# Decays of two linear-attention stages: broadcast sums and per-head activations instead of bf16 matmuls

## The reference, cut to what matters

```python
dt = softplus(x @ Win.T + dt_bias); g = dt * -exp(A_log_bias)
G = cumsum(g, within the chunk)
scores = q_i . k_j
decay = where(i >= j, exp(G_i - G_j), 0)
y_intra = (scores * decay) @ (v * dt)
y_inter = (q * exp(G)) @ state        # of the chunk before
```

## Time and profile before

| | |
|---|---|
| three executions | 2699.6, 2704.6, 2707.73 us (median 2704.6) |
| the profiled execution | 2708.85 us, of which 2707.1 us is the span |
| TensorE busy | 2567.5 us, 95% |
| VectorE, GpSimd, ScalarE busy | 69%, 53%, 50% |
| mean granted TensorE clock | 0.979 |
| moved by DMA | 118.79 MB, mean 44 GB/s |

### The profile page before, as it was taken

How to read it: one execution, slowest core, us unless ns; L and a number is a source line. 1 busy time by engine, 2 the same in 40 slices (tenths; PEclk the granted TensorE clock), 3 DMA queues, 4 the chain that set the end, 5 groups by cost and what they waited for, 6 DMA issues and landing times.

```text
span 2707.1 us, 58907 instructions
## 1 busy us (share of the span) xinstructions
PE 2567.5 (95%) x19678; PEld 2045.6 (76%) x19678; DVE 1862.9 (69%) x2720; ACT 1363.2 (50%) x2492; POOL 1428.0 (53%) x1404
## 2 busy tenths in 40 slices
PE   4999999999999759899999999999999999999989
PEld 3778787787787538677787787777777877877777
DVE  5675766666757568757677767587576777685864
ACT  3434434334334345656665665665566656656621
POOL 1654655546546110457556656475575566564720
PEclk8999999999999769999999999999999999999999
DMA  2010110110110014211111111101111111111011
GB/s 90 24 50 26 35 44 23 44 40 19 52 36 12 17 59 140 78 45 38 50 33 58 34 41 50 38 30 50 45 38 50 33 58 34 42 49 38 19 46 47
DMA packets 72632, 118.79 MB, mean 44 GB/s; under 512 B 10310, under 2 KB 22214, under 8 KB 72373
## 3 DMA queue, kind: packets, MB, share of 16 engines
q1 hardware_dynamic: 72388, 115.61, 13.1%
HBM read 102.92 MB, written 12.65 MB: 43 GB/s over the span
## 4 chain that ended last, share of the span: by engine, by line
PE 52%; DVE 3%; issue 2%; POOL 2%; ACT 0%; DVEq 0%; POOLq 0%; ACTq 0%
PE proj L218 11%; PE proj L220 11%; PE proj L219 11%; PE core_y L1409 5%; PE core_o L1415 2%; PE decay L1471 1%; PE turned L253 1%; DVE mx_acc L1216 1%; PE turned L1439 1%; PE mx_decay L1471 1%; PE mx_normed L1439 1%; PE mx_normed L253 1%; PE core_y L220 1%; PE core_y L218 1%; PE mx_decay L220 1%
## 5 line engine op out<-in xcount | busy, mean ns | idle before, releaser
L218 PE MATMUL proj<-slab_hi,XTL 128*128 128x512 f32 x816 | 355.3, 435 | 0.0
L201 DVE TENSOR_TENSOR slab_lo<-slab_raw,slab_hi 128x512 fp32r<-128x512 f32 (+2 forms) x272 | 245.5, 915 | 148.7 <-ACT slab_hi L192 123.1
L218 PE MATMUL proj<-XTH,slab_lo 128*128 128x512 f32 x736 | 301.2, 409 | 41.0 <-PEq L81 14.4
L220 PE MATMUL proj<-slab_hi,XTH 128*128 128x512 f32 x816 | 321.1, 393 | 0.0
L219 PE MATMUL proj<-slab_lo,XTH 128*128 128x512 f32 x816 | 318.7, 391 | 0.0
L219 PE MATMUL proj<-XTL,slab_hi 128*128 128x512 f32 x736 | 292.9, 398 | 0.0
L220 PE MATMUL proj<-XTH,slab_hi 128*128 128x512 f32 x736 | 292.9, 398 | 0.0
L1670 POOL TENSOR_TENSOR mx_th<-mx_th,mx_acc 128x512 f32<-128x512 f32 x48 | 62.2, 1296 | 363.4 <-ACT mx_th L1569 363.4
L1687 POOL TENSOR_TENSOR mx_gate<-mx_gate,mx_hd 128x512 f32<-128x512 f32 x128 | 167.9, 1312 | 152.1 <-DVE mx_hd L1601 141.1
L218 PE MATMUL proj<-slab_hi,mx_otl 128*128 128x512 f32 x576 | 242.0, 420 | 4.1 <-DVE mx_otl L267 4.1
L220 PE MATMUL proj<-slab_hi,mx_oth 128*128 128x512 f32 x576 | 227.8, 396 | 0.0
(11 more groups left out here) (358 smaller groups left out, 6667.4 us busy)
## 6 DMA issues: line engine op xcount, KB each, us to landing
slab_raw<-in_w_gate SPq DMA_DIRECT2D x64, 256.0 KB, 3.0
slab_raw<-in_w_out SPq DMA_DIRECT2D x64, 256.0 KB, 3.0
slab_raw<-in_w_x SPq DMA_DIRECT2D x60, 256.0 KB, 3.6
slab_raw<-in_w_q SPq DMA_DIRECT2D x32, 256.0 KB, 3.0
slab_raw<-in_w_g SPq DMA_DIRECT2D x32, 256.0 KB, 3.0
slab_raw<-in_w_o SPq DMA_DIRECT2D x32, 256.0 KB, 2.9
bc_scratch<-bc_acc SPq DMA_DIRECT2D x32, 256.0 KB, 2.0
slab_raw<-in_w_bc SPq DMA_DIRECT2D x20, 256.0 KB, 4.4
```

The costliest lines, as they stand in the source:

```text
L201: op = nc.vector.tensor_tensor(K.SL[par][:, c, 0:width], K.RAW[c][:, 0:width], hi, ALU.subtract)
L218: nc.tensor.matmul(to[:, 0:bh.shape[-1]], al, bh, start=(c == 0), stop=False)
L220: mm = nc.tensor.matmul(to[:, 0:bh.shape[-1]], ah, bh, start=False, stop=(c == KC - 1))
```

## The change

G is stored once, in fp32. For each 128 tokens DMA reads a row of the sums of all heads of the round (4 x 128 values, 2 KB) or half (8 x 128, 4 KB) and writes it to all 128 partitions. G is also turned, so that G_j stands as one column per head (`upto`; in layer 0 also `left` = Glast - G). ScalarE makes Relu(G_j - G_i) head by head, with that column as bias, 128 columns at a time, four such activations in place of one; exp follows as before over four heads. The matmuls, the bf16 parts, the row tiles and their setup go. In layer 1 exp is taken while turned tiles are copied out of two banks. In the mixer four tiles of sums are loaded ahead, the first four before the groups. In the attention the bank of the removed matmuls serves as a second bank for turned tiles, so tile t waits for tile t - 2. The program's scratch for dynamic DMA is set to 4096 bytes. The diff, cut to its core (code that is only removed and stands in the listing above is left out in part; `TB`, `GB` and `bank` arguments are passed on likewise elsewhere):

```diff
@@ -132,31 +132,27 @@
+        sums = [nc.dram_tensor(f"sums{i}", s, F32, kind="Internal").ap() for i, s in enumerate(((NB, 2, H0 * P), (NT, P * P)))]
...
+            dt0, upto0, left0 = (mem.enter_context(nc.sbuf_tensor(n, [P, NT, H0], F32)) for n in ("dt0", "upto_sum0", "to_last0"))
...
+            dt1, upto1 = (mem.enter_context(nc.sbuf_tensor(n, [P, NT, P], F32)) for n in ("dt1", "upto_sum1"))
...
-            K.RHS = [mem.enter_context(nc.sbuf_tensor(f"mx_g_rows{i}", [P, HH1, SEQ], BF16)) for i in range(2)]
-            K.LHS = [mem.enter_context(nc.sbuf_tensor(f"mx_j_rows{i}", [P, 2, SEQ], BF16)) for i in range(2)]
@@ -488,20 +475,15 @@
-            sp.dma_start(stage[:, :], d["head_rows"].rearrange("p h n -> p (h n)")).then_inc(S["mx_rows"], 16)
...
-        for i in range(3):
-            for k in range(kinds):
-                sp.wait_ge(av, HEAD + part_made(i, k))
...
-                    sp.dma_start(rows[0][i].rearrange("b h t -> (b h) t"), parts[i][:, :]).then_inc(st, 16)
...
+        sp.wait_ge(vv, HEAD + G_READY)
+        if layer:
+            sp.dma_start(sums.rearrange("t (h i) -> h t i", i=P), G[:, :].rearrange("h (t i) -> h t i", i=P)).then_inc(st, 16)
+        else:
+            for b in range(NB):
+                sp.dma_start(sums[b].rearrange("c (h i) -> h c i", i=P),
+                             G[b * H0:(b + 1) * H0, :].rearrange("h (c i) -> h c i", i=P)).then_inc(st, 16)
+            sp.wait_ge(st, HEAD + 16 * NB)
@@ -509,35 +491,27 @@
-            for i in range(2):
...
+        if layer == 0:
+            for src, ready, bank in ((q, DT_READY, K.PT), (G, G_READY, K.PD), (R, R_READY, K.PO)):
+                pe.wait_ge(vv, HEAD + ready)
+                for i in range(2):
+                    tr = nc.tensor.transpose(bank[:, i * P:(i + 1) * P], src[:, i * P:(i + 1) * P], K.ident[:, :])
...
-    if layer:
-        @block.gpsimd
-        def _(pool):
-            for i in range(2):
...
-                nc.gpsimd.memset(K.LHS[i][:, :, :], 0.0)
...
-                nc.gpsimd.memset(K.RHS[i][:, :, :], 0.0).then_inc(S["mx_zero"], 1)
...
-            for i in range(2):
...
-                nc.gpsimd.memset(K.LHS[i][0:15, :, :], 1.0)
...
-                rows_set = nc.gpsimd.tensor_copy(K.RHS[i][0:15, :, :].rearrange("p h n -> p (h n)"), stage[:, :])
-            rows_set.then_inc(S["mx_set"], 1)
+        else:
+            for use, (src, ready) in enumerate(((q, DT_READY), (G, G_READY))):
+                pe.wait_ge(vv, HEAD + ready)
+                for i, bank in enumerate((K.PT, K.PD)):
+                    if use:
+                        pe.wait_ge(cc, HEAD + i + 1)
+                    for t in range(4):
+                        at = 4 * i + t
+                        tr = nc.tensor.transpose(bank[:, t * P:(t + 1) * P], src[:, at * P:(at + 1) * P], K.ident[:, :])
+                    tr.then_inc(tt, 1)
+            pe.wait_ge(vv, HEAD + R_READY)
+            pe.wait_ge(cc, HEAD + 3)
+            for b in range(NB):
+                tr = nc.tensor.transpose(K.PT[:, b * P:(b + 1) * P], R[:, 2 * b * P:(2 * b + 1) * P], K.ident[:, :])
+            tr.then_inc(tt, 1)
@@ -560,29 +534,23 @@
-                elif dst is dtk:
...
-        for i in range(3):
-            for k in range(kinds):
...
-                nc.scalar.activation(split3[k][i][:, :], ((G, R) if i == 0 else (z, dd))[k][:, :], ACT.Copy).then_inc(av, 1)
-            if layer and i == 0:
-                nc.scalar.activation(e[:, :], G[:, :], ACT.Exp).then_inc(av, 1)
...
-                nc.scalar.activation(w[:, :], R[:, :], ACT.Exp, scale=-1.0).then_inc(av, 1)
...
+        if layer == 0:
+            for k, (dst, bank, sign) in enumerate(((dtk, K.PT, 1.0), (turned[0], K.PD, 1.0), (turned[1], K.PO, -1.0))):
+                act.wait_ge(tt, HEAD + k + 1)
+                nc.scalar.activation(dst[:, :, :].rearrange("p (b i) h -> p i b h", i=2),
+                                     bank[:, 0:2 * P].rearrange("p (i b h) -> p i b h", i=2, b=NB), ACT.Copy, scale=sign).then_inc(cc, 1)
+        else:
+            upto, from_start, to_end = turned
+            for i, bank in enumerate((K.PT, K.PD)):
+                act.wait_ge(tt, HEAD + i + 1)
+                nc.scalar.activation(dtk[:, 4 * i:4 * i + 4, :], bank[:, :].rearrange("p (t h) -> p t h", t=4), ACT.Copy).then_inc(cc, 1)
+            for i, bank in enumerate((K.PT, K.PD)):
+                src = bank[:, :].rearrange("p (t h) -> p t h", t=4)
+                act.wait_ge(tt, HEAD + 2 + i + 1)
+                nc.scalar.activation(from_start[:, 2 * i:2 * i + 2, :], src[:, 1::2, :], ACT.Exp)
+                nc.scalar.activation(upto[:, 4 * i:4 * i + 4, :], src, ACT.Copy).then_inc(cc, 1)
+            act.wait_ge(tt, HEAD + 5)
+            nc.scalar.activation(to_end[:, :, :].rearrange("p b h -> p (b h)"), K.PT[:, :], ACT.Exp, scale=-1.0).then_inc(cc, 1)
@@ -707,18 +667,16 @@
-            sp.dma_start(stage, d["head_rows"][:, 0:REP0, :].rearrange("p h n -> p (h n)")).then_inc(S["at_ld"], 16)
...
-                sp.wait_ge(S["at_set"], HEAD + 1)
-                sp.wait_ge(K.unit_done, HEAD + U + SLOTS * g)
-                sp.dma_start(RHS[0:3, :, :, :], rd[:, :, ds(REP0 * g, REP0), :]).then_inc(S["at_rows"], 16)
-                for k, src in enumerate((nd, md)):
...
+                sp.wait_ge(S["at_e"], HEAD + PAIRS * g)
+                for b in range(NB):
+                    for it in range(2):
+                        src = sums[b, it:it + 1, ds(REP0 * P * g, REP0 * P)].broadcast_to([P, REP0 * P])
+                        sp.dma_start(GB[b][:, it, :, :].rearrange("p h n -> p (h n)"), src).then_inc(S["at_rows"], 16)
@@ -739,11 +697,7 @@
-                nc.tensor.matmul(PS[k % 2][:, :], KH[:, js], QH[:, :, qs], start=False, stop=True)
-                pe.wait_ge(S["at_rows"], HEAD + 48 * (g + 1))
-                pe.wait_ge(S["at_e"], HEAD + PAIRS * g + k - 1)
-                nc.tensor.matmul(PD[k % 2][:, :], LHS[:, int(p == 1), jt * P:(jt + 1) * P], RHS[:, b, :, (it % 2) * P:(it % 2 + 1) * P],
-                                 start=True, stop=True).then_inc(S["at_pair"], 1)
+                nc.tensor.matmul(PS[k % 2][:, :], KH[:, js], QH[:, :, qs], start=False, stop=True).then_inc(S["at_pair"], 1)
@@ -766,18 +720,16 @@
+                        pe.wait_ge(K.ot_lo, HEAD + m - 5 + s)
...
-                            tr = nc.tensor.transpose(K.PT[:, t * P:(t + 1) * P], vT[:, tt * P:(tt + 1) * P], K.ident[:, :])
+                            tr = nc.tensor.transpose(TB[s % 2][:, t * P:(t + 1) * P], vT[:, tt * P:(tt + 1) * P], K.ident[:, :])
...
-                        turn_tile(nc, K, pe, m + t, GT[t % GRING], K.ot_lo if t else S["at_v"], m + t if t else 2 * g + 2)
+                        free, count = (K.ot_lo, m + t - 1) if t >= 2 else (S["at_v"], 2 * g + t + 1)
+                        turn_tile(nc, K, pe, m + t, GT[t % GRING], free, count, TB[t % 2])
@@ -844,15 +796,23 @@
-                            act.wait_ge(S["at_pair"], HEAD + PAIRS * g + k + 1)
+                            b, p = pairs[k]
+                            jt, it = 2 * b + (p == 2), int(p > 0)
+                            act.wait_ge(S["at_rows"], HEAD + 128 * (g + 1))
...
-                                nc.scalar.activation(ex, PD[k % 2][:, :], ACT.Exp).then_inc(S["at_e"], 1)
...
-                                nc.scalar.activation(ex, PD[k % 2][:, :], ACT.Relu, scale=-1.0).then_inc(S["at_rl"], 1)
-                                act.wait_ge(S["at_rl"], HEAD + 8 * g + 2 * pairs[k][0] + (pairs[k][1] == 2) + 1)
-                                nc.scalar.activation(ex, ex, ACT.Exp, scale=-1.0).then_inc(S["at_e"], 1)
+                            alone(act)
+                            for h in range(REP0):
+                                src, head = GB[b][:, it, h, :], ds(REP0 * g + h, 1)
+                                if p == 1:
+                                    ex = nc.scalar.activation(EX[k % 2][:, h, :], src, ACT.Exp, bias=left[:, jt, head])
+                                else:
+                                    rl = nc.scalar.activation(EX[k % 2][:, h, :], src, ACT.Relu, bias=upto[:, jt, head], scale=-1.0)
+                            if p != 1:
+                                rl.then_inc(S["at_rl"], 1)
+                                act.wait_ge(S["at_rl"], HEAD + 8 * g + 2 * b + (p == 2) + 1)
+                                ex = EX[k % 2][:, :, :].rearrange("p h n -> p (h n)")
+                                ex = nc.scalar.activation(ex, ex, ACT.Exp, scale=-1.0)
+                            ex.then_inc(S["at_e"], 1)
@@ -871,14 +831,7 @@
-            nc.vector.memset(LHS[:, :, :], 0.0)
-            nc.vector.memset(RHS[:, :, :, :], 0.0).then_inc(S["at_zero"], 1)
-            dve.wait_ge(S["at_zero"], HEAD + 1)
-            nc.vector.memset(LHS[0:15, :, :], 1.0)
-            dve.wait_ge(S["at_ld"], HEAD + 64)
-            for b in range(NB):
```

(43 more changed lines are left out.)

121 lines of the change are left out of this document (19 added, 102 removed).

## The result

The changed kernel takes 2685.7 us (median of 6 runs, 2680.5 to 2688.2), the one before 2706.2 us beside it (6 runs). The ratio is 0.992, with a 95% interval of 0.991 to 0.993. It is faster, but by 21 us where 67 were forecast; 2638 was off by 48 us and the time lies above the range. The profiled execution took 2688.24 us.

What follows compares the result with a forecast made beforehand. TensorE, busy 95% of the span, was taken to bound the kernel. Terms -24 - 28 - 8 - 6.5 - 5.9 + 5.5 gave -67 us, so 2704.6 became 2638 us, own range 2622 to 2653, with A and B 2608 to 2668.

Steps and rivals of the forecast that it cites:

- Decay matmuls removed, mixer (-50.7): Mixer's score slots: TensorE saves 0.34 or 0.43 us per removed pair of decay matmuls, 50.7 us over sixteen halves.
- ScalarE's price: Decays by head on ScalarE: four 128-column Relus cost 1.32 us against 0.61 for one of 512, 0.7 more.
- ScalarE's lag (+22): Mixer's score slots: gates queue behind longer decays, making TensorE 1.4 us late per half, 22 us over sixteen halves.
- B: Rival, mixer: ScalarE lags more, at 0.36 us per Relu instead of 0.30; +20 us, 2658 us; chance 0.18.
- C: Rival, mixer: ScalarE becomes the bound, slower than before; 2720 us at 0.46 us per Relu; chance 0.03.
- A: Rival, mixer: ScalarE keeps up, so all 50.7 us of removed matmuls stay; 2616 us; chance 0.18.
- D: Rival: broadcasts clog the DMA queue; 2645 us at half the present rate, near 2710 at a quarter; chance 0.04.
- E: Rival: removed matmuls do not pay, hidden behind another chain; only the three openings count; 2690 us; chance 0.07.
- Attention rounds (-24): Attention rounds: each removed set of decay matmuls saves TensorE 0.24 us, x 96, taken as 24 us.
- Attention's start (-6.5): Attention's start: without memsets and casts the first k's rotation, awaited by the third unit, ends 6.5 us sooner.
- mixer's start (+5.5): Mixer's start: four broadcasts issued before the gate slab delay its first chunk, 5.5 us more, bounds 0 and 12.
- Normalisation c (-8) and decay phase (-5.9): Without row-tile setup GpSimd stops slowing VectorE in normalisation c, 8 us; mixer's decay phase has a shorter chain, 5.9 us.

Runs made afterwards that it cites:

- run 1: Changed kernel with one wide Relu or Exp in place of four by head, per-head bias left out, in attention and mixer: 2648.0 us, 0.978.
- Run 9: The kernel of run 4 with HD and TO of tile 1 moved ahead on VectorE, between the two M multiplies of slot r=3: 2646.1 us, 0.978.
- 14: The kernel of Run 9 with the wide Relu and Exp, per-head bias left out, in both phases: 2640.6 us, 0.976.
- run 11: The kernel of Run 9 with GpSimd's XCH of tile 7 ahead of the sums of squares at r=10: 2653.1 us, 0.979.
- run 2: Changed kernel with the broadcasts loaded once ahead of the loops and never again, later decays computed from those rows: 2686.8 us, 0.994.
- run 3: Changed kernel with both the wide Relu or Exp without per-head bias and the broadcasts loaded once: 2653.5 us, 0.982.
- run 4: Changed kernel with gate slabs loaded ahead of the broadcasts on SP, in attention rounds and at the mixer's start: 2664.9 us, 0.985.
- run 7: Changed kernel with GpSimd's row-tile setup (six memsets, two copies) put back in the second decay phase, into tiles nobody reads: 2694.2 us.
- run 6: Changed kernel with one turned bank in the attention again, with the waits of the kernel before: 2680.9 us, 0.991.

## Why the prediction was wrong, and where it was right

*Decay matmuls removed, mixer (-50.7).* The size was right: with ScalarE's work made cheap (run 1) the 16 intervals are 6.5 us a group shorter than before, 52 in all. In the changed kernel only 2.4 us a group of it can be seen.

*ScalarE's price.* Right. 0.30 from one Relu to the next and 0.39 for the last were taken; the rows after say

```profile
1682.73 1.23 ACT L1484 ACTIVATE mx_decay<-mx_g_all,upto_sum 128x128 f32<-128x128 f32 x4
L1484 ACT ACTIVATE decay<-mx_g_all,upto_sum 128x128 f32<-128x128 f32 x380 | 118.1, 370 | 0.0
```

that four take 1.23 us, so with 0.37 for the last they start 0.29 apart, and the mean is 370 ns. One of 512 columns takes 0.60 (run 1), so four cost 0.63 more, where 0.7 was taken. The estimate from the Trainium skill ("ScalarE: Activation LUTs", What ACT_TABLE_LOAD costs), 294 ns apart, agrees with that spacing.

*ScalarE's lag (+22).* This step failed, and it is most of the miss: the mixer's loop was to be 28 us shorter and is 2.9 longer. Two things were wrong in it.

The first is the path. The forecast followed one chain behind ScalarE, tanh and VectorE's gate multiply, and gave it 1.6 us of slack. It did not follow the other, from ScalarE's exp over the M multiply, tile_lo, HD and TO to GpSimd's two products and the turn of tile 1. That one needs 2.6 us of GpSimd behind VectorE's last instruction and ran out first. Run 9 shows it: moving two instructions along it took the wait away. The expected wait for mx_gate of VectorE was short (2.7 us in all in after). By run 1 ScalarE's work costs at least 4.1 us a group, 33 in all, where 22 were taken. That the two sizes are not further apart is luck, for the 22 stood on the wrong chain and on a wrong sum: three units of 2.8, 1.4, 2.1 and 0.9 make 12.8 us, not 12.2, and by the forecast's own steps the lag would then be 1.1 us a half at most instead of 1.7.

The second is a term put at nothing: chains that have nothing to do with ScalarE, and that held TensorE as soon as it came sooner. GpSimd's full queue takes back 1.35 us a group in interval 43, and 0.8 more go in intervals 18, 19 and 42. The turn of the loop takes back what 45 and 47 gained. A cheaper ScalarE left these as they were (runs 1 and 14), and letting XCH go first moved the loss (run 11). That is 2.2 us a group, 17 in all. What ended the waits at 18, 19 and 42, and the 0.3 us at 12 and 36, was not taken apart.

*Rivals.* The "less than 1 us" a half that was put down for B or C came true, but not by their mechanism: the Relu was not mis-sized, the chains behind it were. A fell, and D did (run 2). E's time, 2690, is 4 us from the measured one, and that is chance: the attention paid, the starts did not. But a part of its mechanism is in the traces, since a third of what the 16 intervals gain without ScalarE's lag is hidden behind GpSimd and the other chains (run 3: 4.5 of 6.4 us a group are left).

*Attention rounds (-24).* 17.8 us with the last round, 2.3 a round. Most of the intervals with a decay are 0.24 us shorter, as read from starts, but not the one before the fourth score (interval 15, +0.03), which shrank by 0.27 with the wide Relu: a small lag where nothing was costed. In that run interval 13 grew by 0.44, so the round gained nothing; why is open.

*Attention's start (-6.5) and mixer's start (+5.5).* The forecast of the first looked only at the chain to the third unit, which did start 4.4 us sooner (52.49 instead of 56.91). It left out that eight broadcasts stood ahead of the gate slab on SP, at 1.2 us each. With the slab ahead (run 4) the start is 8.5 us shorter than before. The second had the right cause and was too small: the wait for the slab grew by 8.0 us, and the first eight units by 9.9.

*Normalisation c (-8) and decay phase (-5.9).* Right: 8.1, shown by putting the work back (run 7), and 7.1.

*Two turned banks (0).* Right (run 6).

*Not tested.* The changed program also sets its scratch for dynamic DMA to 4096 bytes, and every run behind the change has this. What it does to the issues on SP is not known.

## What to carry to other kernels

When work goes from the engine that bounds to one that has room on average, follow every chain behind its in-order queue to the bound engine, through all engines, and compare the slack of each: here the longer chain ran out first. Do the same for the engines whose work stays as it is. Their chains become the limit when the bound engine comes sooner, and then a removed instruction wins nothing. Then look for instructions that are ready and stand behind a wait: moving two of them into the gap won nearly as much as the whole change. Such an order is right for one kernel only: the same move cost 22 us in the other. And small transfers on a shared queue have a place in it: put the load that is needed first ahead.

## What was not expected of the hardware

- Eight broadcasts of 256 KB, each of one DRAM row to 128 partitions, kept the issuing queue 9.56 us, 1.2 us each, at the attention's start (over all 64 the issue itself takes 0.33 us at least, 0.43 in the median and 2.09 at most).
- 80 MB more traffic, 23.3% of the DMA engines' span where it was 13.1%, cost at most 1.1 us in a group of 186 (run 2).
- Memsets on GpSimd stretched one VectorE instruction from 0.54 to 4.67 us (run 7).
- At the turn of the mixer's loop VectorE stood idle for 3.1 to 4.6 us (groups 1 to 6, before and after) with nothing to wait for that the profile shows.
